# Gated attention on one core: two groups rounded to fp8 in one chain, one operation per normalised tile, another order on three engines

## The reference, cut to what matters

```python
ln_out = _ln(hidden_states, ln_w, ln_b)
q = _ln(_fp8_linear_pertensor(ln_out, wq, ...).reshape(b, s, g, hpg, d), qln_w, qln_b)
k = _ln(_fp8_linear_pertensor(ln_out, wk, ...).reshape(b, s, g, d), kln_w, kln_b)
v = _fp8_linear_pertensor(ln_out, wv, ...).reshape(b, s, g, d)
core = _gqa(q, k, v).reshape(b, s, nh * d)
...
xout = _gqa(qx, kx, vx).reshape(b, s, nh * d)
cat = jnp.concatenate([core, xout], axis=-1)
catq = _div_clamp_fp8(cat, proj_smooth)
return jnp.einsum('bsi,oi->bso', catq, wproj) * (proj_in_scale * proj_w_scale)
```

## Time and profile before

| | |
|---|---|
| median of 3 runs | 956.44 us (954.7 to 957.12) |
| the profiled execution | 952.76 us, of which 951.0 us are the span from the first to the last instruction |
| granted clock of TensorE, mean | 0.969 |
| TensorE busy over the span | 846.7 us (89%) |
| DVE busy | 710.7 us (75%) |
| ACT busy | 538.9 us (57%) |
| POOL busy | 308.4 us (32%) |

### The profile page before, as it was taken

One profiled execution on the slowest core, in us unless ns is written; L12 is line 12 of the kernel. 1 busy time (PEld: TensorE's weight loads), 2 busy tenths in 40 slices (PEclk: granted clock), 3 DMA queues, 4 the chain that ended last, 5 costly groups with the idle time before them and its releaser, 6 DMA issues. The chain is left out here.

```text
span 951.0 us, 16933 instructions
## 1 busy us (share of the span) xinstructions
PE 846.7 (89%) x6190; PEld 673.9 (71%) x6192; DVE 710.7 (75%) x1135; ACT 538.9 (57%) x1578; POOL 308.4 (32%) x458
## 2 busy tenths in 40 slices
PE   1569988998899889977999999998999997999997
PEld 1557778778878888864777777776555554788885
DVE  7788999999998999798564444444898887466643
ACT  5667776777877787642543333323477775333332
POOL 1233434343433343323322221110333444042320
PEclk9978999999999999978999999999999998999999
DMA  4101010101010100006011111000100002101001
GB/s 159 45 2 67 2 67 2 68 1 68 1 68 2 67 2 24 1 2 238 24 53 53 54 53 53 3 0 0 67 2 1 2 1 68 34 33 46 21 0 45
DMA packets 10922, 35.63 MB, mean 37 GB/s; under 512 B 1248, under 2 KB 5344, under 8 KB 8544
## 3 DMA queue, kind: packets, MB, share of 16 engines
q1 hardware_dynamic: 10704, 34.64, 10.2%
q10 hardware_dynamic: 144, 0.03, 0.0%
HBM read 33.62 MB, written 1.05 MB: 36 GB/s over the span
## 5 line engine op out<-in xcount | busy, mean ns | idle before, releaser
L418 ACT ACTIVATE square<-ps 128x128 bf16<-128x128 f32 x384 | 100.7, 296 | 17.7 <-PE ps L242 17.3
L242 PE MATMUL ps<-wt_hi,xq 128*128 128x512 f32 (+1 forms) x256 | 87.6, 360 | 13.7 <-DVE wt_lo L649 12.4
L1275 POOL TENSOR_TENSOR moe_w_lo<-moe_w_all,moe_w_hi 128x384 fp32r<-128x384 f32 x48 | 53.4, 1150 | 130.2 <-ACT moe_w_hi L1377 130.2
L574 POOL TENSOR_TENSOR rstd<-rstd,half_neg 128x6 f32<-128x6 f32 x64 | 93.0, 1454 | 5.0
L418 ACT ACTIVATION_READ_ACCUMULATOR square<-ps 128x1 f32 x384 | 86.1, 228 | 0.0
L1721 ACT ACTIVATE ca_probs<-ps 128x512 f32<-128x512 f32 x128 | 69.5, 595 | 26.9 <-PE ps L1637 25.9
L242 PE MATMUL ps<-wt_lo,xq 128*128 128x512 f32 (+1 forms) x256 | 83.2, 346 | 0.0
L579 POOL TENSOR_TENSOR probs<-probs,total 128x512 f32<-128x512 f32 x32 | 37.6, 1176 | 139.6 <-DVE total L697 139.6
L1446 DVE TENSOR_TENSOR moe_act_g<-moe_act_g,ps 128x512 f32<-128x512 f32 x48 | 33.1, 689 | 66.4 <-PE ps L1312 66.4
L1393 ACT CAST moe_in_hi<-moe_inner 128x512 fp32r<-128x512 f32 x48 | 29.8, 621 | 89.4 <-DVE moe_inner L1449 77.9
L1312 PE MATMUL ps<-moe_hT_hi,moe_w_hi 128*128 128x512 f32 x192 | 75.8, 395 | 4.4 <-POOL moe_w_lo L1275 4.4
(11 more groups left out here) (226 smaller groups left out, 2499.5 us busy)
## 6 DMA issues: line engine op xcount, KB each, us to landing
moe_w_all<-in_experts SPq DMA_DIRECT2D x8, 1152.0 KB, 5.4
w_in<-in_wt SPq DMA_DIRECT2D x8, 1024.0 KB, 5.7
wp_in<-in_wp SPq DMA_DIRECT2D x8, 512.0 KB, 3.6
ffn_codes<-in_codes SPq DMA_DIRECT2D x8, 384.0 KB, 3.1
ffn_w_scales<-in_code_scales SPq DMA_DIRECT2D x8, 384.0 KB, 3.8
x_rows<-in_x SPq DMA_DIRECT2D x2, 512.0 KB, 4.5
ctx_in<-in_ctxT SPq DMA_DIRECT2D x1, 1024.0 KB, 8.7
context_rows<-in_ctx SPq DMA_DIRECT2D x1, 1024.0 KB, 9.8
```

The lines of the kernel that those rows point to most:

```text
L242: last = mm(ps[:, first + bank, col:col + width], left[:, c, tokens], w[:, c, wcol:wcol + width], start=(j == 0), stop=(j == len(steps) - 1))
L418: last = nc.scalar.activation(square[:, i % 2, j, :], ps[:, bank, (j % 4) * P:(j % 4) * P + P], ACT.Square, scale=float(HD) ** -0.5, accum ...
L574: nc.gpsimd.tensor_tensor(rstd[:, i % 2, :], rstd[:, i % 2, :], k.half_neg[:, 0:6], ALU.pow).then_inc(s["rstd_ready"], 1)
L1275: last = nc.gpsimd.tensor_tensor(w_lo[:, b, cols], w_all[:, b, cols], w_hi[:, b, cols].bitcast(F32), ALU.subtract)
```

## The change

- `quantise` takes a list of groups. In the steps it is called once, with both groups (`quantise(h-2, (0, 1))`), on 128x2048 elements where there were two calls on 128x1024. `y16` and `e16` become one contiguous tile for it. The tail still rounds a group at a time. `rounded(u, r)` gives the new counts of `catq_ready`.
- `normalise` writes six heads by one operation on 128x768 elements across two PSUM banks, and waits for `copy_values` ahead of all of it.
- On the vector engine the merged `quantise` comes right behind `totals(h-1, 0)`; the first part of the work on weights moves behind `normalise` 3, `add_outputs` 0 and 1 move behind `queries` 2 and (in odd steps) behind the second `weights_low`; `output_weights_low` comes behind `totals(h-1, 1)`.
- On TensorE `values(h-2, 1)` comes ahead of `turn_tile` 0.
- On the scalar engine both `weights_high` lie in odd steps, one ahead of `squares` 2, one behind `exponent(h-1, 1)`.

The core of the diff:

```diff
@@ -145,8 +145,8 @@
         total = sb("total", [P, 2, 8], F32)
         probs = sb("probs", [P, 2, 8, SEQ], F32)
         pT = sb("pT", [P, 4, P], F32)
-        y16 = scaled16[:].rearrange("p r c k n -> p r (c k n)")[:, :, 0:HPG * 512].rearrange("p r (h n) -> p r h n", h=HPG)
-        e16 = power16[:].rearrange("p c k n -> p (c k n)")[:, 0:HPG * 512].rearrange("p (h n) -> p h n", h=HPG)
+        y16 = scaled16[:, 0].rearrange("p c k n -> p (c k n)").rearrange("p (r h n) -> p r h n", r=2, h=HPG)
+        e16 = power16[:].rearrange("p c k n -> p (c k n)").rearrange("p (r h n) -> p r h n", r=2, h=HPG)
         catq = sb("catq", [P, 2, HPG, 512], F32R)
         acc = sb("acc", [P, TILES, HID], F32)
         out_scale = sb("out_scale", [P, 1], F32)
@@ -182,6 +182,10 @@
 
         def out_bank(u):
             return PROJ if u == LAST - 1 else CAT_BANK
+
+        def rounded(u, r):
+
+            return u + 1 if u < LAST - 1 else 2 * u - LAST + r + 2
 
         def catq_of(u):
             return xq[:, 0].rearrange("p r (h n) -> p r h n", h=HPG) if u == LAST else catq
@@ -305,7 +309,7 @@
 
             def outputs(u):
 
-                pe.wait_ge(s["catq_ready"], 2 * u + 2)
+                pe.wait_ge(s["catq_ready"], rounded(u, 1))
                 pe.wait_ge(s["wp_lo_done"], u // 2 + 1)
                 for j in range(2):
                     for q in range(2):
@@ -319,7 +323,7 @@
 
             def last_outputs(r):
 
-                pe.wait_ge(s["catq_ready"], 2 * LAST + r + 1)
+                pe.wait_ge(s["catq_ready"], rounded(LAST, r))
                 if r == 0:
                     pe.wait_ge(s["wp_lo_done"], GROUPS)
                     pe.wait_ge(s["shifted"], 2 * UNITS)
@@ -354,10 +358,10 @@
                     turn_probs(h - 2, 1)
                 if is_unit(h - 1):
                     scores(h - 1, 0)
+                if is_unit(h - 2):
+                    values(h - 2, 1)
                 if here:
                     turn_tile(h, 0)
-                if is_unit(h - 2):
-                    values(h - 2, 1)
                 if is_unit(h - 1):
                     scores(h - 1, 1)
                 if here:
@@ -441,7 +445,7 @@
             def take(u, r):
                 if u > 0:
 
-                    act.wait_ge(s["catq_ready"], 2 * (u - 1) + r + 1)
+                    act.wait_ge(s["catq_ready"], rounded(u - 1, r))
                 for j in range(2):
                     act.wait_ge(s["pv_ready"], 4 * u + 2 * r + j + 1)
                     dst = y16[:, r].rearrange("p h (q b s) -> p b q h s", q=4, b=2)[:, j]
@@ -480,8 +484,6 @@
                 if here:
                     keys(h, 1)
                 if h % 2 == 1 and g + 1 < GROUPS:
-                    weights_high(g + 1, 1)
-                if h % 2 == 0 and h > 0 and g + 1 < GROUPS:
                     weights_high(g + 1, 0)
                 if h == 0:
 
@@ -494,11 +496,11 @@
                 if is_unit(h - 1):
                     probs_out(h - 1, 0)
                     exponent(h - 1, 1)
+                if h % 2 == 1 and g + 1 < GROUPS:
+                    weights_high(g + 1, 1)
                 if here:
                     keys(h, 2)
                     keys(h, 3)
-                if h == 0:
-                    weights_high(1, 0)
                 if h == 0:
 
                     act.wait_ge(s["c_in"], 16)
@@ -661,12 +663,9 @@
                 if n >= 2:
 
                     dve.wait_ge(s["tk_ready"], n - 1)
-                nc.vector.tensor_tensor(qn[:, i % 2, 0:4, :], ps[:, bank, :].rearrange("p (h d) -> p h d", h=4),
-                                        rstd[:, i % 2, 0:4].unsqueeze(2).broadcast_to([P, 4, HD]), ALU.mult)
-
                 dve.wait_ge(s["v_copied"], n + 1)
-                nc.vector.tensor_tensor(qn[:, i % 2, 4:6, :], ps[:, bank + 1, 0:256].rearrange("p (h d) -> p h d", h=2),
-                                        rstd[:, i % 2, 4:6].unsqueeze(2).broadcast_to([P, 2, HD]), ALU.mult
+                both = ps[:, bank:bank + 2, :].rearrange("p b (h d) -> p (b h) d", d=HD)
+                nc.vector.tensor_tensor(qn[:, i % 2], both[:, 0:6], rstd[:, i % 2].unsqueeze(2).broadcast_to([P, 6, HD]), ALU.mult
                                         ).then_inc(s["normed"], 1)
 
             def queries(h, i):
@@ -696,13 +695,14 @@
                 dve.wait_ge(s["total_done"], 2 * u + r + 1)
                 nc.vector.reciprocal(total[:, r, :], total[:, r, :]).then_inc(s["rtotal_done"], 1)
 
-            def quantise(u, r):
-
-                dve.wait_ge(s[f"cat_taken{r}"], 2 * u + 2)
+            def quantise(u, rs):
+
+                for r in rs:
+                    dve.wait_ge(s[f"cat_taken{r}"], 2 * u + 2)
                 if 0 < u < LAST:
 
                     dve.wait_ge(s["out_ready"], 2 * u)
-                steps = [0]
+                steps, call = [0], rounded(u, rs[0]) - 1
 
                 def chain(ins):
                     steps[0] += 1
@@ -711,8 +711,9 @@
                     else:
                         ins.then_inc(s["round_step"], 1)
 
-                        dve.wait_ge(s["round_step"], 4 * (2 * u + r) + steps[0])
-                round_to_fp8(nc, chain, y16[:, r], e16, catq_of(u)[:, r])
+                        dve.wait_ge(s["round_step"], 4 * call + steps[0])
+                part = lambda t: t[:, rs[0]:rs[-1] + 1].rearrange("p r h n -> p (r h n)")
+                round_to_fp8(nc, chain, part(y16), part(e16), part(catq_of(u)))
 
             def add_outputs(u, j):
                 dve.wait_ge(s["out_ready"], 2 * u + j + 1)
@@ -737,11 +738,11 @@
                 add_to_rows(half, half)
                 totals(LAST, 0)
                 shift(LAST, 1)
-                quantise(LAST - 1, 0)
+                quantise(LAST - 1, (0,))
                 totals(LAST, 1)
-                quantise(LAST - 1, 1)
-                quantise(LAST, 0)
-                quantise(LAST, 1)
+                quantise(LAST - 1, (1,))
+                quantise(LAST, (0,))
+                quantise(LAST, (1,))
                 for j in range(2):
                     add_outputs(LAST - 1, j)
                 dve.wait_ge(s["out_added"], 2 * LAST)
@@ -767,34 +768,32 @@
                 if h == 0:
 
                     quantise_rows(2)
+                if is_unit(h - 2):
+                    quantise(h - 2, (0, 1))
+                if is_unit(h - 1):
+                    shift(h - 1, 1)
+                if here:
+                    normalise(h, 2)
+                    normalise(h, 3)
                 if ahead and h % 2 == 0:
                     sum_weights(g + 1, 0)
                     centre_weights(g + 1, 0)
                 if ahead and h % 2 == 1:
                     weights_low(g + 1, 0)
-                if is_unit(h - 2):
-                    quantise(h - 2, 1)
-                if is_unit(h - 1):
-                    shift(h - 1, 1)
-                if here:
-                    normalise(h, 2)
-                if is_unit(h - 2):
-                    add_outputs(h - 2, 0)
-                if here:
-                    normalise(h, 3)
-                if is_unit(h - 2):
-                    add_outputs(h - 2, 1)
                 if here:
                     queries(h, 2)
                 if ahead and h % 2 == 1:
                     weights_low(g + 1, 1)
+                if is_unit(h - 2):
+                    add_outputs(h - 2, 0)
+                    add_outputs(h - 2, 1)
                 if ahead and h % 2 == 0:
                     sum_weights(g + 1, 1)
                     centre_weights(g + 1, 1)
+                if is_unit(h - 1) and h < LAST:
+                    totals(h - 1, 1)
                 if h % 2 == 1 and h < LAST:
                     output_weights_low(g)
-                if is_unit(h - 1) and h < LAST:
-                    totals(h - 1, 1)
                 if h == 0:
 
                     quantise_rows(3)
@@ -803,9 +802,6 @@
                         dve.wait_ge(s["c_high"], c + 1)
                         nc.vector.tensor_tensor(ctx_lo[:, c, :], ctx_in[:, c, :], ctx_hi[:, c, :].bitcast(F32), ALU.subtract
                                                 ).then_inc(s["c_low"], 1)
-                if is_unit(h - 1) and h < LAST:
-                    quantise(h - 1, 0)
-
             row_stats(nc, dve, x, stats, mv, s["stats_done"], 0, ready=lambda n: (s[f"x_in{n // 4}"], 16))
 
             dve.wait_ge(s["v_in"], 16)
```

## The result

The changed kernel takes 1019.87 us (median of 4 runs, 1015.62 to 1023.08), the kernel before 955.57 us (4 runs, 954.5 to 957.12). The ratio is 1.0679, with a 95% interval of 1.0652 to 1.0705: **64 us slower**. The profiled execution took 1017.88 us, its span 1016.1. Two lines of its page come first, then two groups of its costliest instructions (columns: line, engine, operation, out<-in, count | busy us, mean ns | idle us just before, and what ended it).

What follows compares the result with a forecast made beforehand. The vector engine was taken to set the pace, in a ring through all four engines. 952.76 + 47 (longer steps) + 28 (half clock) = 1027.8 us, plus 3.7 for the median: 1031 us, range 992 to 1056.

Steps and rivals of the forecast that it cites:

- What is saved: Vector engine: merged rounding saves 0.83 us a unit, one-operation normalising 0.05 us a tile; together 1.0 to 1.8 us a step.
- First walk: Step 9 up to `outputs`: it may start at offset 17.38 instead of 16.14, TensorE standing still 2.4 us ahead of it.
- Second walk: Step 9 from `outputs` to the next step: `values(h-1, 0)` waits 3.2 us for the second `add_outputs`; step 4.05 us longer.
- some 3 us in 12 or more steps: Expected sign on TensorE: its longest waits are `values` for the vector engine's `acc`, this long and this often.
- The longer ring: Dependencies through all four engines lengthen steps 2 to 15 to 377.6 us against 330.65: +47 us, 10 us either way.
- The clock: TensorE at half clock after its waits ahead of `values` and `outputs`: 2.0 us in each of 14 steps, +28 us.
- clock at 0.9 or below: Expected sign in the changed kernel: TensorE's granted clock over the attention steps falls to this level.
- The power: POOL's work for tile 2, ahead of `normalise` 2: starts after L101 and the addition, takes 1.32 us, ends at 18.75.
- The vector engine keeping the pace: Rival: the vector engine still bounds the steps and gets its savings, 1.8 us a step: 931 us, chance 0.05.
- The clock staying up: Rival: TensorE's new waits come but its clock does not drop: 1003 us, chance 0.20.
- half clock behind both waits at full price: Rival: half of a step's products slow and slack used up, 3.5 us a step instead of 2.0: 1052 us, chance 0.13.
- The page: Skill guidance set against the forecast: grouping nine operations less a step on the vector engine saves 0.8 us, 11 us in 14 steps.

Runs made afterwards that it cites:

- the kernel with short fillings: The changed kernel plus two idle products on TensorE ahead of `outputs` and two ahead of `values(h-1, 0)`, results unused: 1004.80 us, ratio 1.0539.

## Why the prediction was right

The forecast was 1031 us, within 992 to 1056, from a longer ring and half clock; the measured 1019.87 lies in it, and the cause is the one foretold. By its steps:

- **What is saved.** The 0.05 us a tile were the right size: over 64 tiles that is 3.2 us, and the normalisation alone gave 2.3 (0.9965, 0.9946 to 0.9984). The merging's 0.83 us a unit were not seen as time anywhere, as said: the vector engine's busy time fell by 24.6 us, and no run shows more than the normalisation's part of it as time.
- **First walk.** `outputs` was to start at 17.38 after the step's first projection. In step 8 it starts at 266.84 - 247.97 = 18.87, of which 1.42 us is half clock on the first projection (tile 0 takes 3.53 us, tile 2 at full clock 2.11). Without it: 17.45, 0.07 from the forecast. The chain from L97 to the end of L101 took 6.13 us, where the earlier trace rows has 5.73 without the overlap taken off; I had allowed 0.3 for POOL, it was 0.40, and L97 alone had 0.39 of it. My wait of 2.4 us ahead of `outputs` should have been 2.3 by my own offsets (1.07 + 17.38 - 16.14); measured are 1.86 to 2.52.
- **Second walk.** Step 8 is an even one with the short projection: 26.2 us forecast, 27.68 measured, 1.42 of them clock. TensorE's wait ahead of `values` was to be 3.2 us in step 9. It was 2.58 there, behind `outputs` that ran partly at half clock; with the clock held up the filling and the wait behind it make 1.88 + 1.14 = 3.0. The longest wait of all steps was 3.5 and the mean 2.2 (30.9 us over 14), so the sign "some 3 us in 12 or more steps" did not come true.
- **The longer ring**, +47 us: with the clock held up steps 2 to 15 take 378.52 us, where my walks add up to 377.6, so +47.9 against the 330.65 before. The single kinds of step fit too: even short ones 26.0 us (forecast 26.2), odd short ones 26.7 (27.05), even long ones 26.9 (27.1), odd long ones 28.3 (28.2). TensorE's idle time in the windows gives 44.6. This is the term that carried the forecast, and it held.
- **The clock**, +28 us: measured 14 in the steps (392.60 - 378.52) and 15 in all. This is the **mis-sized term**. I let nearly every step have half clock behind the wait for `acc` and some behind the wait for `catq`, 2.0 us of it on the ring. The trace shows one stretch a step on average: 0.94 over 392.60 us, at two levels 1.00 and 0.50, makes 12% or 47 us at the lower one, 3.4 us a step (before, 0.98 over 330.65 us: 13 us). Half of the difference is 17 us, as the busy time said. But they are unevenly spread. Windows over the start of each step show 0.58 to 0.73 in steps 2, 4, 5, 8, 9, 12 and 14 and 1.00 in the others, windows over `outputs` 0.56 to 0.69 in steps 2, 5, 6, 9, 11, 12 and 14. The starts of steps 7 and 8:

```profile
219.73:224.00 4.27, 4.27 (x20) 3.48 (x19) 1.41 (x3) 3.21 (x17) 1.04 (x1) 1.00 0.00 0
247.97:252.00 4.03, 4.03 (x17) 3.55 (x16) 0.69 (x1) 1.87 (x7) 1.59 (x1) 0.58 0.53 199
```

So what I had "nearly always" came behind six of 13 waits, and the 0.92 us that I put on `values` itself came hardly at all: the block right behind the wait took 1.16 us, its time at full clock, in 11 of 14 steps, and where it was slow it was the projection behind it. A stretch inside `outputs`, as in step 9 at 296.00, is partly taken up again by the wait for `acc` that follows. So my "clock at 0.9 or below" did not come true, and the total came out 11 us high. What decides between a slow and a full start is not shown.
- **The wait I left out.** `values(h-2, 1)` for `probs_out` is 14.8 us in all, 13.7 of them in the steps. My first walk placed it rightly (6.55; measured 8.06, less the clock's 1.42 is 6.64), but did not say that TensorE stands still ahead of it; in the sum it was covered, since the old wait for tile 0 at this place (1.49 us in the earlier trace rows, 23.2 us over 14 steps) went away. Undoing this order gave back 10.6 us.
- **The power.** I had it start behind L101. It starts within 0.1 us of L101, at 264.60, and then takes 3.37 us instead of 1.32, so it ends at 20.00 after the step's start, where I had 18.75 plus the clock's 1.42, 20.17. Two errors of opposite sign: that this place came out right is luck. In the steps 3, 7 and 11 the addition ahead of it has the long form (2.12 us) and the power its 1.32.
- **The rivals.** The vector engine keeping the pace (931 us) is refuted: it idles 86.2 us ahead of the tiles. The clock staying up (1003 us) is what the kernel with short fillings showed as a possible world, 1004.80 us; half clock behind both waits at full price (1052) did not occur.
- **The page.** "Perfetto Trace Analysis" of the Trainium skill, section "Optimizing Scalar/DVE Operations", says that grouping helps a saturated engine and that breaking work up can help where the vector engine is not saturated but makes bubbles on other engines. This case's runs side with the second sentence, although the engine was busy for 22.23 of 23.00 us before: merged alone, +33 us.

What stays open: how the 5 us between 69.5 and 64.3 are shared, how much half clock costs the kernel before, and what the two moves that had no run of their own in the changed kernel (`output_weights_low` behind `totals`, the scalar engine's `weights_high`) add by themselves.
